# Window attention in rounds of two tile shapes: a new order of the TensorE groups, with half of the on-chip copies issued by GpSimd

## What is computed

```
x = x + zca(group_norm(x))       # 16 groups of 4 channels: mean, 4x4 covariance,
                                 # its inverse square root, applied to the 4 channels
x = x + attention(group_norm(x)) # batch norm, then windows of 49 pixels, 16 heads of 16:
    attn = softmax(q @ k.T / 4); v = relu(tok @ v_w.T); o = attn @ v
```

## Time and profile before

| | |
|---|---|
| runs | 506.59 us median of 3 |
| the profiled execution's own time | 506.08 us |
| its span | 504.4 us |
| TensorE busy | 449.0 us, 89% |
| VectorE, ScalarE, GpSimd busy | 336.2, 294.7, 190.7 us |
| stage 1, until about | 60.8 us |
| stage 2, until about | 89.4 us |
| stage 3, until about | 119.7 us |
| stage 4, until | 504.4 us |

### The profile page before, as it was taken

How to read it: one execution, slowest core, us unless ns; L and a number is a source line. 1 busy time by engine, 2 the same in 40 slices (tenths; PEclk the granted TensorE clock), 3 DMA queues, 4 the chain that set the end, 5 groups by cost and what they waited for, 6 DMA issues and landing times. The chain is left out here.

```text
span 504.4 us, 38739 instructions
## 1 busy us (share of the span) xinstructions
PE 449.0 (89%) x17474; PEld 361.0 (72%) x17474; DVE 336.2 (67%) x1077; ACT 294.7 (58%) x515; POOL 190.7 (38%) x158
## 2 busy tenths in 40 slices
PE   8999814985878999999999999999999999999964
PEld 8898713321666788888887887888788788878853
DVE  1544478883356777777777777777777777777744
ACT  2322210564656677767767776777677677767731
POOL 4071000002124455445544554454455445544512
PEclk9999956999699999999999999999999999999988
DMA  8970000001111414243241424324142433414232
GB/s 300 418 315 3 3 0 1 1 0 40 60 70 66 128 66 143 81 127 121 94 136 64 135 87 130 109 99 143 64 129 87 136 96 104 145 71 127 80 85 66
DMA packets 31567, 52.08 MB, mean 103 GB/s; under 512 B 6176, under 2 KB 21024, under 8 KB 30624
## 3 DMA queue, kind: packets, MB, share of 16 engines
q1 hardware_dynamic: 31520, 51.50, 30.3%
HBM read 12.95 MB, written 12.85 MB: 51 GB/s over the span
## 5 line engine op out<-in xcount | busy, mean ns | idle before, releaser
L309 POOL TENSOR_TENSOR X<-X,otok 128x392 f32<-128x392 f32 x63 | 107.3, 1703 | 193.0 <-DVE otok L713 193.0
L680 DVE TENSOR_REDUCE rmax<-ps 113x16 bf16<-113x784 f32 x128 | 120.8, 944 | 36.3 <-PE ps L866 36.2
L891 PE MATMUL ps<-diag,qk_all 64*49 64x98 f32 x4096 | 130.1, 246 | 0.2 <-ACT prob_all L360 0.2
L360 ACT ACTIVATE prob_all<-ps 113x784 f32<-113x784 f32 x128 | 105.7, 826 | 36.0 <-PE ps L898 34.7
L891 PEld LDWEIGHTS ps<-diag,qk_all 64*49 64x49 f32 x4096 | 110.6, 122 | 21.3 <-issue 15.2
L898 PE MATMUL ps<-mdiag,sel 64*49 64x98 bf16 x2048 | 112.2, 203 | 0.2 <-DVE mdiag L688 0.2
L303 POOL TENSOR_SCALAR xs<-X,affined 128x392 f32<-128x392 f32 x64 | 69.4, 1085 | 90.8 <-DVE affined L671 77.0
L375 ACT ACTIVATE vst<-ps 49x256 f32<-49x256 f32 x256 | 97.0, 379 | 11.4 <-PE ps L851 8.0
L367 ACT ACTIVATE qk_all<-ps 128x784 f32<-128x784 f32 x64 | 52.8, 825 | 71.9 <-PE ps L835 71.9
L697 DVE RECIPROCAL rden<-ps 128x98 f32<-128x98 f32 x64 | 49.4, 771 | 37.2 <-PE ps L914 37.2
L898 PEld LDWEIGHTS ps<-mdiag,sel 64*49 64x49 bf16 x2048 | 66.6, 101 | 0.5 <-issue 0.4
(11 more groups left out here) (161 smaller groups left out, 363.6 us busy)
## 6 DMA issues: line engine op xcount, KB each, us to landing
diag<-qk_all SPq DMA_DIRECT2D x256, 98.0 KB, 2.0
out<-X SPq DMA_DIRECT2D x30, 392.0 KB, 4.7
X<-x_in SPq DMA_DIRECT2D x7, 1024.0 KB, 16.1
X<-x_in SPq DMA_DIRECT2D x7, 544.0 KB, 16.9
X<-x_in SPq DMA_DIRECT2D x4, 256.0 KB, 3.7
out<-X SPq DMA_DIRECT2D x2, 294.0 KB, 3.8
X<-x_in SPq DMA_DIRECT2D x2, 192.0 KB, 4.6
out<-X SPq DMA_DIRECT2D x2, 98.0 KB, 2.4
```

Of the source, the lines that this page charges most:

```text
L309: g.tensor_tensor(rows_of(u), rows_of(u), otok[u % 2][:].rearrange("p k a s -> p k s a"), ALU.add).then_inc(S["x_ready"], 1)
L360: a.activation(prob[u % 3][0:ROW, k].rearrange("p h g x j q -> p h (g x j q)"), ps[0:ROW, B_ST:B_ST + 2, 0:8 * POS], ACT.Exp, scale=SCALE) ...
L680: v.tensor_reduce(rmax[u % 3][0:ROW, :, 8 * k:8 * k + 8], ps[0:ROW, B_S:B_S + 2, 0:8 * POS].rearrange("p h (v q) -> p h v q", q=POS), AX.X ...
L891: mm(ps[64 * e:64 * e + POS, B_ST + hh, col:col + 2 * POS], qk[u % 3][r, g, k, 2 + x_, :], diag[u % 3][r, e::2, g, k, x_, :], start=True, ...
```

## The change

It has five parts.

```diff
+AT_SUMS, AT_AFFINE = 3, 10
+AT_QK, AT_S, AT_MT = (15, 18), (24, 27), 30
...
-                for j in range(4):
+                for j in range(2):
                     sp.dma_start(diag[u % 3][j::4, j]...).then_inc(diag_in[u % 3], 16)
...
+            def spread(u):                      # on GpSimd
+                after(pool, "qk_ready", u + 1)
+                after(pool, "st_ps", KH * (u - 2))
+                for j in range(2, 4):
+                    g.dma_start(diag[u % 3][j::4, j]...).then_inc(diag_pool[u % 3], 16)
...
                 if has(i + 3):
                     normalise(i + 3)
-                if 0 < i < UNITS:
-                    add(i - 1)
+                if has(i + 2):
+                    spread(i + 2)
+                if 1 < i <= UNITS:
+                    add(i - 2)
...
-                    chain(v.tensor_tensor(prods[:, 0], rows(Z), cols(Y), ALU.mult))
-                    chain(v.tensor_reduce(ms[:], prods[:, 0], AX.X, ALU.add))
-                t_step = v.scalar_tensor_tensor(ms[:], ms[:] if n > 0 else Y, ...)
+                    chain(v.tensor_tensor(zy[:, n, :, :, 0:ZG], rows(Z), cols(Y), ALU.mult))
+                    t_step = v.tensor_reduce(T, zy[:, n], AX.X, ALU.add)
...
-            warm_up(20)
+            warm_up(8)
...
+            def body(i, at, later, times):
+                u, s, z = i, i + 1, i - 1
+                if has(s):
+                    landed(s, times)            # two waits: SyncE's and GpSimd's copies
+                    scores_for_max(s, 0)
+                if has(u):
+                    need("prob0", at)
+                    scores_for_exp(u, 1)
+                if has(s):
+                    need("max0", at)
+                    scores_for_max(s, 1)
+                    need("qk_ready" if s < UNITS - 1 else "v_ready", at)
+                    project_v(s)
+                if has(z):
+                    sum_weights(z)
+                if has(s):
+                    need("max1", at)
+                    turn_max(s)
+                    need("prob1", later)
+                if has(z):
+                    weigh_values(z)
+                if has(s):
+                    scores_for_exp(s, 0, later) # waits for mdiag inside
+                if has(i + 3):
+                    need("xs_ready", later)
+                    need("v_ready", later)
+                    project_qk(i + 3)
```

More of the change, by code:

```diff
@@ L179, in conv_preact_kernel @@
         MT = 8 * POS
-        B_MIX = (2, 4)
+        B_MIX = [4 if n % 2 == 0 else 6 if n < MIX - 4 else 2 for n in range(MIX)]
         B_GRAM = (4, 5)
@@ L196, in conv_preact_kernel @@
         CREDIT = {"v_ready": 2, "prob0": 2, "prob1": 3, "max0": 1, "max1": 1, "mdiag_ready": 2, "rden_ready": 4, "o_ready": 4}
-        diag_in = [S["diag0"], S["diag1"], S["diag2"]]
+        diag_in, diag_pool = [[S[f"{n}{b}"] for b in range(3)] for n in ("diag", "pdiag")]
         block = ctx.enter_context(nc.Block())
@@ L212, in give, with mixed @@
                 eng.sem_inc(S[n], CREDIT[n])
+        act_both = {3, 7}
+        by_dve = [n for n in range(MIX) if n not in act_both]
+        def mixed(eng, n, m):
+            if m == 0 or n in act_both:
+                after(eng, "mix_act", n + 1)
+            else:
+                after(eng, "mix_dve", by_dve.index(n) + 1)
         def place(u):
@@ L379, in keep_v @@
                 ins.then_inc(S["v_ready"], 1)
+            act.wait_ge(S["dd_ready"], 1)
             act.wait_ge(S["zeros_ready"], 3)
-            for i in range(-2, UNITS + 1):
+            for n in range(MIX):
+                if n == 4:
+                    act.wait_ge(S["var2_ready"], 1)
+                    a.activation(std[:], var[:], ACT.Sqrt).then_inc(S["std2_ready"], 1)
+                if n == AT_QK[0]:
+                    keep_qk(0)
+                if n == AT_QK[1]:
+                    keep_qk(1)
+                if n == AT_S[0]:
+                    keep_v(0)
+                mix(n)
+                if n == MIX - 4:
+                    mixed(act, MIX - 5, 0)
+                    mixed(act, MIX - 5, 1)
+                    a.activation(ps[:, B_ST:B_ST + 2, :], diag[0][:].rearrange("p j g k a s -> p (j g k a s)")[:, 0:1024].rearrange(
+                        "p (b c) -> p b c", b=2), ACT.Copy).then_inc(S["psum_zero"], 1)
+            for i in range(0, UNITS + 1):
                 u, w = i, i + 2
+                if has(u):
+                    weights(u, 0)
                 if has(w):
@@ L386, in _ @@
                 if has(u):
-                    weights(u, 0)
+                    weights(u, 1)
                 if has(i + 1):
                     keep_v(i + 1)
-                if has(u):
-                    weights(u, 1)
         @block.vector
@@ L610, in _ @@
             dve.wait_ge(S["dd_ready"], 1)
-            mix(0)
             dve.wait_ge(S["ag_ps"], 1)
@@ L648, in _ @@
             dve.wait_ge(S["var2_ready"], 1)
-            for n in range(14, 18):
-                mix(n)
+            mix(4)
             dve.wait_ge(S["std2_ready"], 2)
@@ L672, in _ @@
                           ).then_inc(S["affine_ready"], 1)
-            for n in range(28, MIX):
-                mix(n)
+            mix(9)
+            mix(10)
+            pair_matrix(5)
+            mix(11)
+            pair_matrix(6)
+            mix(12)
+            pair_matrix(7)
             def maximum(u, k):
@@ L717, in _ @@
             dve.wait_ge(S["zeros_ready"], 3)
-            for i in range(-1, UNITS + 1):
+            for n in range(13, MIX):
+                if n in AT_S:
+                    maximum(0, AT_S.index(n))
+                if n == AT_MT:
+                    spread_max(0)
+                mix(n)
+            for i in range(0, UNITS + 2):
                 s, z = i + 1, i - 1
+                if has(z - 1):
+                    divide(z - 1)
                 if has(s):
                     maximum(s, 0)
-                if has(z):
-                    invert(z)
-                if has(s):
                     maximum(s, 1)
```

286 lines of the change are left out of this document (132 added, 154 removed).

## The result

The changed kernel took **512.55 us** (median of 4 runs, 512.32 to 515.01) against 507.41 for the kernel before in the same comparison: ratio 1.0123, 95% interval 1.0091 to 1.0156. It is slower by 1.2%. The forecast was 495.0, with 481 to 504 as its range and 0.07 for slower; the time lies outside the range. The profiled spans are 510.5 and 504.4 us.

A forecast was written before the change was run, and what follows sets the result against it. The prediction took TensorE to bound the loop, with waits on ScalarE and VectorE in the new round. Start -1.9, root -1.3, mix and fill -9.2, loop +1.2 and tail 0 made -11.2: 495.0 us, range 481 to 504.

The forecast's parts named there:

- Turn 0.05: TensorE's round: the turn's matmuls take 0.05 us, with weigh following directly, in a round of 5.57 us.
- the two VectorE chains: Loop round: max k=0 to max k=1, and max k=1 to turn, each at least 1.56 us through VectorE's maximum.
- stalls ahead of exp k=1: Loop round: TensorE stands 0.33 us before exp k=1, waiting for ScalarE's weights k=0.
- waits over both maxima: Loop round: TensorE waits for VectorE's maxima, 0.18 us ahead of max k=1 and 0.11 ahead of turn.
- the floors below: Loop round: 4.95 us for TensorE's work alone and 5.17 for VectorE; over the loop -37 and -23.6 us.
- VectorE's floor of 5.17: Loop round: VectorE's 4.14 us of work plus its waits for max k=1 and turn give at least 5.17 us.
- Issue: GpSimd's copies in the loop: issuing one DMA costs 1.0 us, between 0.59 and 1.98.
- rivals with late copies: Loop: copies land 4.4 to 5.0 us after qk, adding 0.1 to 0.4 a round; 502.4 us at 5.69; chance 0.16.
- GpSimd as the bound: Loop: slow DMA issue makes GpSimd's round exceed 5.57 us; at 1.6 us per issue, 521 us; chance 0.08.
- the same links in both orders: 0, with bounds of 1: From unit 63's exp k=0 to the end: 13.0 us before, change 0, at most 1 us either way.
- Start, root, mix: Before the loop: start -1.9 us, root -1.3, mix and fill -9.2; unit 1's exp k=0 at 124.8 against 137.18.
- 32.6: Mix and fill: 32.6 us from the first mix to unit 0's exp k=0.

The follow-up runs named there:

- sp_copies: The changed kernel with all four copies issued by SyncE again, none by GpSimd: 503.77 us, ratio 0.9934.
- prob1_sp: The changed kernel with the wait for the weights k=1 moved ahead of the turn and all four copies issued by SyncE: 492.44 us, ratio 0.9734.
- prob1_first: The changed kernel with only the wait for the weights k=1 moved ahead of the wait for the maxima and the turn: 501.66 us, ratio 0.9901.

## Why the prediction was wrong

The profiled execution missed its forecast by 510.5 - (504.4 - 11.2) = 17.3 us: 9.1 from unit 1 to unit 63 (11.0 too much in the rounds, less 1.9 in the few rounds off that pace), 7.0 at the end, 1.2 before unit 1.

**The round, the step that failed: "Turn 0.05".** The sum priced the turn by its four short matmuls and let weigh follow at once, although the change puts `need("prob1", ...)` between them. It named neither this wait nor a price for it; the wait was satisfied, but its handling, a register instruction (0.09) and a nop (0.11), stands on the path. The step measured 0.23: +0.18 x 62 = 11.2 us, and moving the wait alone gives 10.9 us back. The other steps were off by little: the two VectorE chains 1.54 and 1.55 (forecast 1.56), weigh with its change 0.83 (0.87), exp k=0 0.89 (0.85), project 0.67 (0.68), together 5.71. The mean of 5.75 is longer since 12 of 57 rounds have an exp k=1 of about 1.13 in place of 1.00; with SyncE's copies none has. The earlier trace rows held the warning: the turn took 0.36 there, which the prediction itself put down as "shape change and two satisfied waits included", and then dropped. That reading was right: behind that turn stand a register instruction and two nops, and nothing is waited for. As an upper bound for the turn, 0.36 would have made the loop 62 x 0.31 = 19 us longer, a rival of its own.

**The chains.** The stalls ahead of exp k=1 and the waits over both maxima came where they were forecast, and the floors below were real: moving work into the stall shortened the typical round to 5.33. VectorE's floor of 5.17 wasn't reached.

**The copies.** Issue 0.54 us (forecast 1.0, bounds 0.59 and 1.98) and landing 2.0: both are cheaper than forecast, and the wait on a DMA was 0.4 us once. Part 2 isn't free in the loop, though: without it the round is 0.03 shorter (`sp_copies`) or 0.065 (`prob1_sp` against `prob1_first`), 2 to 4 us in all, against a forecast of 0. The rivals with late copies and with GpSimd as the bound didn't occur. The Trainium skill, "DMA: Bandwidth & Descriptors", gives a longer time to the first byte for GpSimd's path, about 1 us against 0.6. No run here shows the first byte; from issue to landing the rows show 2.0 us (GpSimd) against 2.1 (SyncE), no difference. Where the copies stand matters far more: ahead of add, in the new order, 0.4 us of waits; behind it, in the old one, 41.5.

**The tail: "the same links in both orders: 0, with bounds of 1".** It measured +7.0. Of that 5.5 is GpSimd's DRAIN, a price of part 2 that no row of before could show, and that the prediction hadn't bounded, because it looked for the cost of a DMA only where it is issued. 1.45 are issue gaps of TensorE in the last rounds, which have moved there.

**Start, root, mix.** The statistics end 2.2 us earlier (forecast 1.9), the root takes 0.9 less (1.3), and first mix to unit 0's exp k=0 takes 34.0 (32.6): 86.28 to 120.27. In all 11.2 of 12.4 forecast. The missing 1.4 us of the mix are TensorE's clock, on which the prediction is silent: the first 24 mix matmuls took 4.20 us at a granted clock of 0.50. In the six kernels with the clock at 1.00 there, first mix to unit 0's exp k=0 takes 32.0 to 32.2 us in place of 34.0, and the sum would have been 0.4 to 0.6 too long. So its 32.6 was close, and that this execution missed it was a matter of the clock.

**The chances.** The rival on the other side was GpSimd as the bound, at 0.08. The true mechanism of the slower side, a satisfied wait in a bad place, wasn't among the rivals, and neither was a longer end.

## What to carry to other kernels

A wait that is always satisfied is still made of instructions: here a register instruction for its count and a nop, about 0.1 us each. They were hidden only where TensorE waited for something else anyway or where its sequencer was ahead of the matmuls: behind the values (0.57 us) a nop cost nothing, behind four short matmuls 0.1 to 0.2 us every round, and two more nops and a register instruction behind the weighted values 0.29 us. When reordering, read the sequencer's instructions between the groups and not only the idle time, and price each wait whose predecessor is short. When an engine begins to issue DMAs, look also at what it does at the program's end. Look at the granted clock ahead of each stage before a difference is put down to an edit. And count the rounds left outside a loop: three of them cost 8.5 us (493.60 to 485.10), as much as shortening the round by 0.14 us gains.

## What the runs showed of the hardware that was not expected

- GpSimd's closing DRAIN takes 1.8 us plus 0.082 us for every DMA of 32 packets that GpSimd has issued in the program (1.85, 6.99 and 12.23 us for 1, 64 and 128), regardless of when.
- On TensorE, behind four short matmuls, the register instruction of a satisfied wait costs about 0.09 us (step 0.11 against 0.02) and a nop about 0.10 (0.12 against 0.02); both together make the step 0.22. The wait itself costs almost nothing.
- In kernels that are the same up to there, the clock in the first mix steps was granted at 0.50 in one execution and 1.00 in another, and the time to the first maximum was 25.99 or 24.04 us.
- One more wait and nop in TensorE's loop can make it fetch its code again and again (1.57 MB in place of 0.39) and cost 137 us; the same instructions two groups earlier in the loop don't. What decides this wasn't found.
